# We's broadcast row read from a PSUM bank: a one-core GNN, attention and MoE block

## The reference, cut to what matters

```python
xn = layernorm(x)                                   # x: 1250 x 512
for l in range(4):                                  # 40000 edges, sorted by dst
    e = edge_weight @ We[l] + be[l]                 # edge_weight: 40000 x 1, We[l]: 1 x 512
    m = relu(xn[src] + e)
    agg = segment_sum(m, dst)
    h = batch_norm(((1 + eps) * xn + agg) @ W1[l] + b1[l])
    xn = relu(relu(h) @ W2[l] + b2[l])
x = x + gnn + mix(layernorm(x))                     # mix: linear attention, 8 heads of 64
x = x + ffn(layernorm(x))                           # one of 8 experts a row
# mix: q, k = elu(.)+1, v; kv = sum_s k v; z = 1/(q . sum_s k); out = (q kv z) @ Wp + bp
```

## Time and profile before

| | us |
|---|---|
| median of 3 runs | 1782.31 (1780.24 to 1782.49) |
| profiled execution, its own time | not told apart from its span |
| profiled execution, span | 1786.3 |
| PE busy | 1471.2 (82%) |
| DVE busy | 1317.5 (74%) |
| POOL busy | 1095.1 (61%) |
| ACT busy | 938.3 (53%) |

### The profile page before, as it was taken

How to read it: one execution, slowest core, us unless ns; L and a number is a source line. 1 busy time by engine, 2 the same in 40 slices (tenths; PEclk the granted TensorE clock), 3 DMA queues, 4 the chain that set the end, 5 groups by cost and what they waited for, 6 DMA issues and landing times.

```text
span 1786.3 us, 22128 instructions
## 1 busy us (share of the span) xinstructions
PE 1471.2 (82%) x6948; PEld 647.6 (36%) x6948; DVE 1317.5 (74%) x2538; ACT 938.3 (53%) x1076; POOL 1095.1 (61%) x1080
## 2 busy tenths in 40 slices
PE   2686988886887888888898898989978988898797
PEld 2232333332333333332443333333433333334465
DVE  6789798888547888777576888787578888775634
ACT  1444444444334666666536666665456666663321
POOL 4777677777215777777146777774167777770033
PEclk8897999997889999999999999999999999999889
DMA  6676667777237777777357777774477777866343
GB/s 217 199 201 197 171 196 203 200 223 234 75 95 213 214 212 213 207 204 208 85 159 223 226 228 211 209 236 131 121 223 222 225 219 213 244 196 229 147 146 112
DMA packets 119078, 343.23 MB, mean 192 GB/s; under 512 B 20696, under 2 KB 24876, under 8 KB 118702
## 3 DMA queue, kind: packets, MB, share of 16 engines
q0 software_dynamic: 85248, 278.41, 54.9%
q1 hardware_dynamic: 32302, 60.78, 10.6%
q10 hardware_dynamic: 1408, 2.56, 0.4%
HBM read 323.61 MB, written 19.96 MB: 192 GB/s over the span
## 4 chain that ended last, share of the span: by engine, by line
PE 48%; DVE 16%; ACT 12%; POOL 11%; issue 7%; DMA 5%; DVEq 1%; POOLq 0%; SPq 0%; ACTq 0%
PE ps L1791 43%; ACT ring L1585 10%; POOL ring L815 9%; DVE ring L1001 9%; DMA ring<-x_table,idxT 4%; PE ps L1856 3%; DVE lg L1056 1%; POOL ring L866 1%; DVE aggT L1417 1%; DMA aggT<-pair_table,token_i 1%; DVE onehot L995 1%; DMA x_table<-ring 1%; DMA mix<-in_edge_weight 1%; DVEq L1043 0%; PE ps L2221 0%
## 5 line engine op out<-in xcount | busy, mean ns | idle before, releaser
L815 POOL DMA_INDIRECT ring<-x_table,idxT x1014 | 1038.5, 1024 | 518.3 <-issue 292.8
L1001 DVE SCALAR_TENSOR_TENSOR ring<-we_bc,wT,ring 128x512 f32<-128x512 f32 x1014 | 688.6, 747 | 69.7 <-DMA ring<-x_table,idxT 65.1
L1585 ACT ACTIVATE ring<-ring 128x3072 f32<-128x3072 f32 x161 | 444.7, 2762 | 281.0 <-DVE ring L1001 281.0
L1791 PE MATMUL ps<-ring,onehot 128*32 128x512 f32 x2028 | 362.2, 653 | 196.0 <-ACT ring L1585 192.1
L1631 ACT ACTIVATE zT<-ps 128x512 f32<-128x512 f32 x336 | 189.8, 601 | 142.3 <-PE ps L1791 139.5
L1791 PE MATMUL ps<-ring,zT 128*128 128x512 bf16 x1080 | 262.4, 382 | 0.8
L1791 PE MATMUL ps<-zT,xT 128*32 128x512 f32 (+2 forms) x752 | 258.6, 619 | 1.6 <-DVE mix L1191 1.6
L1056 DVE TENSOR_REDUCE lg<-ps 128x128 f32<-128x512 f32 x208 | 143.2, 688 | 113.9 <-PE ps L1856 71.1
L1791 PEld LDWEIGHTS ps<-ring,onehot 128*32 128x32 f32 x2028 | 72.0, 113 | 380.1 <-ACT ring L1585 239.7
L1791 PE MATMUL ps<-w,zT 128*125 128x512 f32 (+2 forms) x320 | 146.5, 621 | 20.2 <-ACT zT L1709 20.2
L1791 PE MATMUL ps<-aggT,w 128*128 128x512 f32 (+1 forms) x384 | 143.6, 524 | 6.9 <-DVE aggT L1057 3.6
(11 more groups left out here) (310 smaller groups left out, 1283.1 us busy)
## 6 DMA issues: line engine op xcount, KB each, us to landing
ring<-x_table,idxT POOLq DMA_INDIRECT x1014, 4.1
zT<-slot_table SPq DMA_DIRECT2D x36, 312.5 KB
w<-in_L_gnn_W SPq DMA_DIRECT2D x8, 1024.0 KB, 10.9
ring<-in_L_ffn_W SPq DMA_DIRECT2D x16, 512.0 KB, 9.9
x_table<-ring SPq DMA_DIRECT2D x24, 250.0 KB
ring<-in_x SPq DMA_DIRECT2D x1, 2304.0 KB
x_table<-ring SPq DMA_DIRECT2D x9, 256.0 KB
stage<-in_x ACTq DMA_DIRECT2D x9, 256.0 KB
```

The source lines that it names most:

```text
L815: gp.indirect_dma_start(out=to, out_offset=None, in_=table[:, :], in_offset=bass.IndirectOffsetOnAxis(ap=idx, axis=0)).then_inc(done, 16)
L1001: ins = v.scalar_tensor_tensor(out=at[:, u, :], in0=we_bc[:, :], scalar=wT[:, c, u:u + 1], in1=at[:, u, :], op0=ALU.mult, op1=ALU.add)
L1585: a.activation(at, at, ACT.Relu).then_inc(relu_done, 1)
L1791: return nc.tensor.matmul(o, lhsT, rhs, start=start, stop=stop)
```

## The change

`we_bc` is copied once a layer by ACT into a PSUM bank (`terms_copy`: ps5 in layer 0 from step 15 on, ps6 in layers 1 to 3), and `add_tiles` reads the terms from there. To free the banks, `TAKES` is 2 in every mixed layer; the key-value sums take one bank (eight matmuls of 64 x 65 for four of 128 x 129, a tile); v goes through ps7; the attention's numerators go into ps7 alone, and its denominators are made ahead, in layer 0's steps 47 to 51 (`norms`: 40 matmuls of two columns, one pair of reciprocals on DVE); the transposes between layers use ps4, ps5, ps7, ps1; layer 0's early sums have 3 banks for 4.

```diff
-    def takes(l):
-        return 2 if l == 1 else 3
+    TAKES = 2
...
-        return tiles[:takes(l)], tiles[takes(l):]
+        return tiles[:TAKES], tiles[TAKES:]
...
+    TERMS_FROM = QS + 3
+    act_jobs[QS + 1].append(("terms", 0))
+
+    NORMS = ((46, range(0, 6)), (47, range(6, 7)), (48, range(7, 8)), (49, range(8, 9)), (50, range(9, NT)))
...
+        def terms_bank(l):
+            return ps[6] if l in MIXED else ps[5]
...
         def take_bank(l, T):
-            return ps[4 + T % takes(l)]
+            return ps[4 + T % TAKES]
...
+                terms = terms_bank(l) if l in MIXED or j >= TERMS_FROM else we_bc
+                if l not in MIXED and j == TERMS_FROM:
+                    v.wait_ge(terms_ready, 1)
                 for u in tiles:
-                    ins = v.scalar_tensor_tensor(out=at[:, u, :], in0=we_bc[:, :], scalar=wT[:, c, u:u + 1],
+                    ins = v.scalar_tensor_tensor(out=at[:, u, :], in0=terms[:, :], scalar=wT[:, c, u:u + 1],
                                                  in1=at[:, u, :], op0=ALU.mult, op1=ALU.add)
...
+            def terms_copy(l):
+
+                a.wait_ge(we_loaded, l * 16 + 16)
+                a.activation(terms_bank(l)[:, :], we_bc[:, :], ACT.Copy).then_inc(terms_ready, 1)
...
                 for c in range(KD):
-                    at = slice(c % 2 * (P + 1), (c % 2 + 1) * (P + 1))
-                    ins = mm(ps[6 + c // 2][:, at], k_rows[0:r, c * P:(c + 1) * P], v_rows[0:r, c, :], t == 0 and c % 2 == 0, t == NT - 1 and c % 2 == 1)
+                    for h in range(2):
+                        ins = mm(ps[6][h * HD:(h + 1) * HD, c * (HD + 1):(c + 1) * (HD + 1)], k_rows[0:r, c * P + h * HD:c * P + (h + 1) * HD],
+                                 v_rows[0:r, c, h, :], t == 0 and c == 0, t == NT - 1 and c == KD - 1)
...
+                if kind == "norms":
+                    r = rows(i)
+                    if i == 0:
+                        pe.wait_ge(v_ready, NT)
+                        pe.wait_ge(kvblk_ready, 1)
+                    for f in range(KD):
+                        at = i * NORM + f * 2
+                        ins = mm(v_bank[0:r, at:at + 2], mix[:, i, f * P:f * P + r], kvblk[:, f, P:], True, True)
+                    ins.then_inc(norms_done, 1)
```

More of the change, by code:

```diff
@@ L224, in build_gps_block @@
     dve_jobs[0].append(("weights", 0))
+    TERMS_FROM = QS + 3
+    act_jobs[QS + 1].append(("terms", 0))
+    NORMS = ((46, range(0, 6)), (47, range(6, 7)), (48, range(7, 8)), (49, range(8, 9)), (50, range(9, NT)))
+    for at, tiles in NORMS:
+        pe_jobs[at] += [("norms", t) for t in tiles]
+    dve_jobs[51].append(("norms", 0))
     for m, at in enumerate((3, 5, 7)):
@@ L487, in build_gps_block @@
         we_loaded = sem("we_loaded")
+        terms_ready = sem("terms_ready")
+        norms_done = sem("norms_done")
         be_loaded = sem("be_loaded")
@@ L632, in split_before @@
             return MIXED.index(l) * NT
+        FIRST_BANKS = (ps[3], ps[4], ps[6])
         def early_bank(l, e):
             if l not in MIXED:
-                return (ps[3], ps[4], ps[6], ps[7])[e % KD]
-            return ps[7] if e <= KD else ps[e - 1]
+                return FIRST_BANKS[e % len(FIRST_BANKS)]
+            return ps[7] if e <= KD else (ps[4], ps[5], ps[3])[e - KD - 1]
+        def terms_bank(l):
+            return ps[6] if l in MIXED else ps[5]
+        v_bank = ps[7]
+        turn_bank = (ps[4], ps[5], ps[7], ps[1])
         def take_bank(l, T):
-            return ps[4 + T % takes(l)]
+            return ps[4 + T % TAKES]
         pick_bank, pick_fold = ps[3], ps[7]
@@ L1088, in messages @@
             def messages(l):
-                v.wait_ge(we_loaded, l * 16 + 16)
+                if l in MIXED:
+                    v.wait_ge(terms_ready, l + 1)
+                else:
+                    v.wait_ge(we_loaded, 16)
                 if l in MIXED:
@@ L1200, in job @@
                     if i == 0:
-                        step(v.memset(v_rows[:, :, P:], 1.0))
+                        step(v.memset(v_rows[:, :, :, HD:], 1.0))
                         v.wait_ge(mixw_loaded, 80)
@@ L1210, in job @@
                     step(v.memset(kvblk[:, :, :], 0.0))
[L1211 to L1216, removed]
+                    kvp = ps[6][:, 0:KD * (HD + 1)].rearrange("p (a e) -> p a e", e=HD + 1)
+                    for h in range(2):
+                        q = slice(h * HD, (h + 1) * HD)
+                        v.tensor_copy(kvblk[q, :, q], kvp[q, :, 0:HD])
+                        ins = v.tensor_copy(kvblk[q, :, P + h:P + h + 1], kvp[q, :, HD:])
                     step(ins)
@@ L1221, in job @@
                     v.wait_ge(nd_done, i + 1)
[L1222 to L1229, removed]
+                    v.tensor_tensor(mix[0:r, i, :].rearrange("p (h e) -> p h e", e=HD), pick_fold[0:r, :].rearrange("p (h e) -> p h e", e=HD),
+                                    norms[0:r, i, :].unsqueeze(2).to_broadcast([r, NORM, HD]), ALU.mult).then_inc(att_ready, 1)
+                if kind == "norms":
+                    v.wait_ge(norms_done, NT)
+                    of = v_bank[:, 0:NT * NORM].rearrange("p (t h) -> p t h", t=NT)
+                    v.reciprocal(norms[:, 0:NT - 1, :], of[:, 0:NT - 1, :])
+                    step(v.reciprocal(norms[0:LAST, NT - 1, :], of[0:LAST, NT - 1, :]))
                 if kind == "proj":
@@ L1650, in first_pieces @@
                     high_piece(l, t)
+                    if t == 1:
+                        terms_copy(l)
                 high_piece(l, NT - 1)
@@ L1721, in beside @@
                         a.activation(by_tile(mix[:, i, :])[:, :, 0:rows(i)], by_tile(pick_fold[:, :])[:, :, 0:rows(i)], ACT.Copy).then_inc(att_columns, 1)
+                    if kind == "terms":
+                        a.wait_ge(q_ready, QS)
+                        terms_copy(l)
                     if kind == "q":
@@ L1887, in early_sums @@
                     pe.wait_ge(pick_relu, QB[l + 1] * SW)
-                elif e >= KD:
-                    pe.wait_ge(h_copied, early_before(l) + e - KD + 1)
+                elif e >= len(FIRST_BANKS):
+                    pe.wait_ge(h_copied, early_before(l) + e - len(FIRST_BANKS) + 1)
                 first_layer(l, e // KD, e % KD, early_bank(l, e)).then_inc(h_done, 1)
@@ L1902, in take_rows @@
                     pe.wait_ge(pick_ready, QB[l] + q + 1)
-                if at >= takes(l):
-                    pe.wait_ge(pick_relu, at - takes(l) + 1)
+                if at >= TAKES:
+                    pe.wait_ge(pick_relu, at - TAKES + 1)
                 if q == 0:
@@ L2036, in job @@
                     r = rows(i)
-                    if i > 0:
+                    if i == 0:
+                        pe.wait_ge(left_known, 2)
+                    else:
                         pe.wait_ge(v_ready, i)
                     for k in range(KD):
-                        ins = mm(ps[5][0:r, :], xT[:, k, i * P:i * P + r], wv[:, k, :], k == 0, k == KD - 1)
+                        ins = mm(v_bank[0:r, :], xT[:, k, i * P:i * P + r], wv[:, k, :], k == 0, k == KD - 1)
                     ins.then_inc(v_done, 1)
```

22 lines of the change are left out of this document (11 added, 11 removed).

## The result

The changed kernel takes 1803.6 us (median of 4 runs, 1796.8 to 1807.2) beside 1782.4 us (4 runs) for the kernel before: ratio 1.0104, 95% interval 1.0078 to 1.0131. It is slower by 21 us. The profiled execution spans 1805.4 us, where the earlier trace rows had 1786.3.

What follows compares the result with a forecast made beforehand. POOL's gathers were taken to set the pace where nothing else is slower, ACT and PE in layer 1, a chain through projection and DVE in layers 2 and 3. −7 + 0 + 19 + 0.5 = +12.5 us, median 1795, range 1787 to 1805.

Steps and rivals of the forecast that it cites:

- Two take banks in layers 2 and 3: Layers 2 and 3: one take moves behind each fold, ACT's next relu then waits for PE; +19 us, 13.6 to 24.4.
- The steps carried over from layer 1: Layers 2 and 3: steps of 7.33 us, 7.98 with two later takes, 1.34 more per early sum; 135.2 for steps 20 to 36.
- A step with a projection: Layers 2 and 3, steps 2 to 19: next relu after 8.67 us by PE alone, 8.8 or 9.05 over DVE.
- Layer 0's gathers: Layer 0, mainly chunks 25 to 52: terms from PSUM stop additions holding POOL's gathers; −7 us, between −9 and 0.
- The denominators: End of layer 0: 80 PE passes, 10.6 us, mostly hidden in PE's waits for the relu; +0.5 us.
- Layer 1: Layer 1: its chain runs through ACT and PE, with neither POOL nor DVE in it, and stays; 0 us.
- The rest: Key-value sums, We copies, v's first tile, attention on DVE and removed semaphore increments: put at 0.
- What POOL waits for: All layers: POOL issues a gather 0.30 us after the last and never rests while a layer runs.
- Faster, as the banks don't bind: Rival: layers 2 and 3 keep their pace and gain from POOL; −14 us in all, 1768 us; chance 0.10.
- Slower still by 65 ns an addition: Rival: DVE's additions 65 ns longer with a PSUM source, paid in layers 2, 3 and partly 0; 1806 us; chance 0.08.

Runs made afterwards that it cites:

- c4: The changed kernel with every term read from SBUF again, the two take banks and other moves kept, on chip 3: 1811.1 us, 1.0163 of the kernel before.
- c2: The changed kernel itself, run again as a control on chip 3: 1804.2 us, 1.0114 of the kernel before.
- e1: The kernel before with only two take banks in layers 2 and 3 too, terms still from SBUF, on chip 2: 1.0034 of the kernel before.
- e1b: The kernel before with only two take banks in layers 2 and 3 too, repeated on chip 7: 1.0063 of the kernel before.
- c1: The changed kernel itself, run again as a control on chip 4: 2123.8 us, 1.0403 of the kernel before.
- e2: The changed kernel with every term read from SBUF again, all else as changed, on chip 2: 2027.3 us, 1.0036 of the kernel before.

## Why the prediction was right, point by point

Its time (1795) is 8.6 us under the result, its range and its sign held, and its main step is the one that decided. Of the 8.6, 1.4 are the take banks, 1.7 layer 0 and 3.5 the rest, which had been put at nothing; the last 2 are that the new profile lies 1.8 us above its median, where the old one lay 4.0 above.

- **Two take banks in layers 2 and 3, +19 (13.6 to 24.4): +20.4** in the first pair of profiles, +28 on chip 3, of which 3.4 are two slower steps of layer 3 and 4.3 a quicker profile of before (268.7 and 268.8 us for 271.0 and 270.8). The steps carried over from layer 1 are exact: chunks 20 to 37 take 1230.11 − 1094.89 = 135.2 us in layer 2 and 135.2 in layer 3, for 135.2 worked out. A step with a projection takes 8.98, within 8.67 to 9.05, and by DVE's route. Chunks 2 to 20 take 145.9 for 142.5 to 144.4, as one step of each layer is 9.68 us; in layer 2's the granted clock is 0.77 from 951.0 to 958.5 us.
- **Layer 0's gathers, −7 (−9 to 0): −11.0** between the two kernels that differ in nothing else. The direction and the cause were right and the size was too small: I took chunks 25 to 52 and what those gathers lost over 946 ns in one profile (999 ns on average); with the terms in SBUF the same stretch of chip 3 had 1012 and 1016, with PSUM 960. The lower bound of my own sum, −9, was no bound.
- **The denominators, +0.5: +5.2** for them and all else of the change in layer 0. This is the step that failed, and in its overlap. The 48 passes ahead of step 47 were counted at 6.3 us (0.13 each, from rows at the higher clock) and took 7.1 (c4), 7.9 (after) and 10.2 (c2) at granted clocks of 0.74, 0.67 and 0.50. Their cover, PE's wait for the relu, was named but not measured: the gap was 4.2 to 5.2 us. The passes of the four later steps had no cover at all, as PE doesn't wait there. The miss on the gathers and this one cancel, which is luck: −6.5 was forecast for layer 0, and −4.8 and −5.8 measured.
- **Layer 1, 0: 0.** 274.6 and 274.6 us, and on chip 3 273.2 before and 274.6 in both changed kernels; a quicker POOL behind a loop of ACT and PE gave nothing. The same holds for layers 2 and 3, now that they have that loop.
- **The rest, 0: +3.5 us** between and behind the layers. Part of it may be the clock: in the first 10 us of the weights' products ahead of layer 2 (from 884.28 before, from 878.88 after) it is granted at 0.73, for 0.83 before. Single stretches of the two profiles of before differ by 1.3 to 2.8 us, so what the moved banks cost there can't be told from nothing.
- **What POOL waits for.** The prediction has POOL never rest while a layer runs. In the kernel before it already waits for PE, for 35.4 us in all; no sum rests on this.
- **The rivals.** Faster, as the banks don't bind: refuted by the table of steps. Slower still by 65 ns an addition: 744 ns after, 747 with SBUF terms. The Trainium skill's overheads of 58 and 120 cycles (VectorE: DVE Perf Modes, The TRN2 errata) don't show in this operation. Its rule on the read interface that DVE and GpSimd share (SBUF — State Buffer, Who interferes with whom) is borne out by intervention, 1012 against 960 ns.

## What to carry to other kernels

A buffer freed for one engine is taken from another: before moving something into a PSUM bank, find what that bank's count lets overlap, and look in the same trace for a stage that already runs with one bank less. Here layer 1 was that stage, and for chunks 20 to 37 its steps gave the new length to the tenth of a microsecond. A shorter instruction pays only in the stages where its engine sets the pace: 68 ns a gather, 1014 times, gave 11 us of the 69 on chip 3. Work that is put into another engine's wait needs both lengths, that of the wait and its own at the clock granted there.

## What the runs showed that was not expected

On chips 2, 4, 6 and 7 TensorE stops without waiting for anything that the trace shows, at places of its program that in part recur: 25 of the 71 stops of over 1 us in e1 stand at the same weight load in e1b, on another chip. The changed kernel in layer 2, at the same place of its matmul stream, at first (after), then on chip 4 (c1):

```profile
1189.47 2.32 PE L1821 MATMUL ps<-ring,zT 128*128 128x512 bf16 x9
```

```profile
1411.99 1.24 PE L1821 MATMUL ps<-ring,zT 128*128 128x512 bf16 x5
...
1416.78 0.82 PE L1821 MATMUL ps<-ring,zT 128*128 128x512 bf16 x3 [3.55 <-issue]
```

In c1 long stops often lie 110 weight loads apart (behind load 2871, 2981 and 3091; 4369, 4479, 4589 and 4699): the loads' engine idles 4 to 8 us there, and 0.53 us at the same places in the first profile. PE's waits by releaser, chip 4 (c1), where chip 3 has 0.5 us of it for the same kernel (c2):

```profile
PE ps L1821 <- issue: 246.9, 110, 8.1
```

The trace doesn't show what the stops wait for. Such regular places suggest the fetching of instructions, but its own DMA packets don't bear that out: their number is the same in c1 and in the first profile but for one, and in 23 of c1's 25 stops of over 3.5 us none of them is under way. By the line above the sum is 134 us in the SBUF-term kernel (e2), 150 to 193 with two banks alone, 166 and 187 with three banks in layers 2 and 3, 140 and 151 with the takes first.

The stops aren't all that is slow there. Layer 1's steps from chunk 2 to 37, whose program two banks alone leave as it was, take 333.0 us in e1 for 274.6, with 26.5 us of stops at issue and a mean granted clock of 0.92 for 0.99; the rest is put down to PE's other waits. The kernel before wasn't profiled on such a chip, so what part of a ratio is stops can't be told. The ratios themselves don't carry over: a kernel that is 1.011 on chip 3 was 1.040 on chip 4, and one that is 1.016 was 1.0036 on chip 2. Why the chips differ, and why the stops grow in some kernels, stays open. Read first how long TensorE stands at issue, before a ratio of two kernels is put down to their difference.
